# Attention over 64 graphs: scores six units ahead of the projections' count, a group of its own for the first projections, Q's weights from ScalarE's queue

## What is computed

```python
x = normal(64, 128, 512); adj = 0/1 (64, 128, 128), diagonal 1; Wq, Wk, Wv, Wo (512, 512), biases
q, k, v = heads(x @ Wq + bq), heads(x @ Wk + bk), heads(x @ Wv + bv)
scores = einsum('bhqd,bhkd->bhqk', q, k) / sqrt(32);  scores = where(adj[:, None] == 0, -inf, scores)
attn = softmax(scores);  out = einsum('bhqk,bhkd->bhqd', attn, v) @ Wo + bo
y = layernorm(x + out)          # no scale, no shift, eps 1e-5
```

## Time and profile before

| what | value |
|---|---|
| times of the runs | 904.38 us median of 3 (902.62 to 906.38) |
| the profiled execution | 906.47 us, of which its span (first to last instruction) is 904.7 us |
| mean granted TensorE clock | 0.984 |
| TensorE matmul busy | 870.5 us (96%) |
| VectorE busy | 810.5 us (90%) |
| ScalarE busy | 689.5 us (76%) |
| GpSimd busy | 272.3 us (30%) |

### The profile page before, as it was taken

The page is one execution under the profiler, slowest core; times in us unless marked ns, Lnnn a source line. Parts: engine busy times, 40 slices in busy tenths (PEclk is TensorE's granted clock), DMA queues, the critical chain, the costliest instruction groups (busy, mean ns, idle before and its releaser), DMA issues.

```text
span 904.7 us, 32198 instructions
## 1 busy us (share of the span) xinstructions
PE 870.5 (96%) x11784; PEld 607.9 (67%) x11784; DVE 810.5 (90%) x3449; ACT 689.5 (76%) x1745; POOL 272.3 (30%) x386
## 2 busy tenths in 40 slices
PE   6989999999999999999999999999999999999954
PEld 4666667776667777666777666777766677766632
DVE  5779999999999999999999999999999999999983
ACT  5777778877788877787887778877778788777761
POOL 0113233332233332323333223333232333322222
PEclk9999999999999999999999999999999999999967
DMA  8267899879789988799887779898889998778773
GB/s 302 59 129 123 161 182 183 164 152 153 151 171 179 177 169 153 136 167 182 181 159 172 144 148 169 178 177 161 145 159 159 182 178 171 156 141 158 149 135 93
DMA packets 362414, 144.98 MB, mean 160 GB/s; under 512 B 340752, under 2 KB 344848, under 8 KB 361872
## 3 DMA queue, kind: packets, MB, share of 16 engines
q1 hardware_dynamic: 362256, 142.93, 81.6%
HBM read 42.21 MB, written 16.78 MB: 65 GB/s over the span
## 4 chain that ended last, share of the span: by engine, by line
PE 93%; DVE 4%; DMA 1%; issue 1%; ACT 0%; SPq 0%; POOL 0%; POOLq 0%; DVEq 0%
PE proj_ps L605 76%; PE score_ps L605 9%; PE av_ps L605 8%; DVE masked L492 1%; DVE p_pair L479 1%; DMA w_land<-weights 1%; DVE y L518 0%; DMA aT<-a_pair 0%; DVE stats L521 0%; DVE v_parts L465 0%; DVE a_pair L458 0%; ACT probs L407 0%; ACT p_pair L417 0%; SPq L253 0%; DVE inv_sum L501 0%
## 5 line engine op out<-in xcount | busy, mean ns | idle before, releaser
L407 ACT ACTIVATE probs<-masked,minus_max 128x128 f32<-128x128 f32 x1024 | 327.0, 390 | 167.2 <-DVE minus_max L492 166.3
L492 DVE CUSTOM_DVE_ANT_0 masked<-score_ps,mask 128x128 f32<-128x128 f32 x1024 | 237.4, 287 | 45.1 <-PE score_ps L605 39.8
L479 DVE SCALAR_TENSOR_TENSOR p_pair<-probs,p_pair 128x512 f16<-128x512 f32 x256 | 197.6, 772 | 1.3 <-ACT p_pair L417 1.0
L605 PE MATMUL proj_ps<-wo_hi,aT 128*128 128x512 f16 x512 | 166.3, 387 | 2.7 <-DMA aT<-a_pair 1.6
L417 ACT ACTIVATE p_pair<-probs 128x512 f16<-128x512 f32 x256 | 161.3, 630 | 8.1
L225 POOL TENSOR_TENSOR xT_lo<-xT_raw,xT_hi 128x512 f16<-128x512 f32 x60 | 69.9, 1165 | 317.0 <-ACT xT_hi L370 317.0
L605 PE MATMUL proj_ps<-xT_hi,wq_hi 128*128 128x256 f16 x512 | 141.7, 277 | 8.6 <-DVE wq_lo L573 7.6
L605 PE MATMUL proj_ps<-xT_lo,wq_hi 128*128 128x256 f16 x512 | 141.2, 276 | 0.0
L605 PE MATMUL proj_ps<-xT_hi,wq_lo 128*128 128x256 f16 x512 | 141.2, 276 | 0.0
L605 PE MATMUL proj_ps<-xT_hi,wk_hi 128*128 128x256 f16 x512 | 140.2, 274 | 0.0
L605 PE MATMUL proj_ps<-xT_hi,wk_lo 128*128 128x256 f16 x512 | 139.6, 273 | 0.0
(11 more groups left out here) (58 smaller groups left out, 1521.2 us busy)
## 6 DMA issues: line engine op xcount, KB each, us to landing
xT_raw<-x_cols SPq DMA_DIRECT2D x32, 512.0 KB, 4.5
x_in<-x_rows SPq DMA_DIRECT2D x32, 512.0 KB, 5.4
out<-y SPq DMA_DIRECT2D x64, 256.0 KB, 4.6
adj_in<-adj SPq DMA_DIRECT2D x32, 128.0 KB, 2.9
pT<-p_pair SPq DMA_TRANSPOSE x256, 3.4
w_land<-weights SPq DMA_DIRECT2D x2, 1024.0 KB, 7.5
w_land<-weights SPq DMA_DIRECT2D x4, 256.0 KB, 4.8
x_res<-weights SPq DMA_DIRECT2D x1, 1024.0 KB, 9.3
```

The source lines that it names most:

```text
L407: ins = act.activation(probs[s % 2][:, j * S:(j + 1) * S], masked[s % 2][:, j], ACT.Exp, bias=minus_max[s % 2][:, j:j + 1], scale=-1.0)
L479: dve.scalar_tensor_tensor(out=p_pair[s % NT][:, HW:2 * HW], in0=probs[s % 2][:], scalar=P_UP, in1=p_pair[s % NT][:, 0:HW], op0=ALU.mult, ...
L492: ins = dve.tensor_tensor_reduce(masked[s % 2][:, j], score_ps[j][:, s % HC], mask[par][:, s // KC], -EXP_SCALE, 3.0e38, ALU.add, ALU.min, ...
L605: return pe.matmul(dst, lhsT, rhs, start=first, stop=last)
```

## The change

- TensorE's order is shifted: step (g, s) now scores unit 8g+s+6, attends unit 8g+s+2, and the other engines follow at fixed distances (`MAXED` 5, `TURNED` 4, `NORMED` 1). The distances between a unit's scores, its maximum, its transposes and its attention are those of before.
- The loop begins at g = -1. In that group the projections of group 0 are the banks, and the first scores stand in its step 2. The order of banks is Q0, K0, Q1, K1, V0, V1, Y of graph 1 of the group before, Y of graph 0 of this group; the last group has the scores of two units left, and six attentions.
- On VectorE `low_part_bank` is in steps 1 to 6, `low_part_attn` in 1 and 3, `make_mask` in 2, `y_and_moments` in 7 and 0. On ScalarE the high parts of attention's output are in 0 and 3, those of x in 2 and 4. On GpSimd `normalize` is in 0 and 1, `residual` in 2 and 4, the low part of x in 3 and 5. Wo's parts are made in step 7 of group -1 and steps 0 to 2 of group 0.
- Q's weights (four DMAs) are issued by ScalarE ahead of its first instruction, the others still by SyncE.
- The counters without a reader are gone.

```diff
-    TASKS = ((Q, 0), (Q, 1), (K, 0), (K, 1), (V, 0), (Y, 0), (V, 1), (Y, 1))
-    LAG = 3
+    TASKS = ((Q, 0), (K, 0), (Q, 1), (K, 1), (V, 0), (V, 1), (Y, 1), (Y, 0))
+    SCORED, MAXED, TURNED, ATTENDED, NORMED = 6, 5, 4, 2, 1
...
+    def at_work(g, s, ahead):
+        u = unit(g, s) + ahead
+        return [divmod(u, SLOTS)] if 0 <= u < NG * SLOTS else []
...
             load_xT(0)
-            load_w("q")
             sp.dma_start(b_raw[:], b_cols[:]).then_inc(bias_loaded, 16)
...
-                pool.sem_inc(gpsimd_goes, 1)
...
         def _(pool):
...
             def group(g, par):
                 for s in range(SLOTS):
-                    if s == 1 and at_least(g, 2):
+                    if s == 0 and g >= 2:
                         normalize(g - 2, 1)
+                    if s == 1 and g >= 1 and has_next(g):
+                        normalize(g - 1, 0)
...
-                    if s in (3, 6) and has_x_next2(g):
+                    if s in (3, 5) and has_x_next2(g):
...
-                    if s == 7 and at_least(g, 1):
-                        normalize(g - 1, 0)
...
         def _(act):
...
+            for c, loaded in enumerate(w_loaded["q"]):
+                act.dma_start(w_raw["q"][:, c:c + 1], w_dram[0, :, c:c + 1]).then_inc(loaded, 16)
...
         def _(dve):
...
-                dve.sem_inc(vector_goes, 1)
...
             def group(g, par):
                 for s in range(SLOTS):
-                    masked_max(g, s, par)
-                    before, slot = back(g, s, 1)
-                    if exists(before):
-                        low_part_probs(before, slot)
-                    if s > 0 and TASKS[s - 1][0] != Y and has_next(g):
+                    for unit_g, t in at_work(g, s, MAXED):
+                        masked_max(unit_g, t, unit_g % 2)
+                    for unit_g, t in at_work(g, s, TURNED):
+                        low_part_probs(unit_g, t)
+                    if 1 <= s <= N_SPLIT and has_next(g):
                         low_part_bank(g + 1, *TASKS[s - 1], nxt)
-                    if s in (2, 4) and at_least(g, 1):
-                        low_part_attn(g - 1, s // 4)
+                    if s == 1 and g >= 1:
+                        low_part_attn(g - 1, 1)
+                    if s == 3 and g >= 0:
+                        low_part_attn(g, 0)
...
-                    if s == 0 and at_least(g, 2):
-                        y_and_moments(g - 2, 1, par)
-                    if s == 6 and at_least(g, 1):
-                        y_and_moments(g - 1, 0, nxt)
...
+                    if s == (0 if has_next(g) else 3) and g >= 1:
+                        y_and_moments(g - 1, 0, nxt)
+                    if s == SLOTS - 1 and g >= 1 and has_next(g):
+                        y_and_moments(g - 1, 1, nxt)
...
         def _(pe):
...
             def group(g, par):
                 for s in range(SLOTS):
+                    if has_next(g):
+                        step_bank(g, s, par)
+                        for unit_g, t in at_work(g, s, ATTENDED):
+                            attend(unit_g, t, unit_g % 2)
+                        for unit_g, t in at_work(g, s, SCORED):
+                            scores(unit_g, t, unit_g % 2)
+                        continue
...
+            for g in range(-1, NG):
+                group(g, g % 2)
+            step_bank(LAST, 7, LAST % 2)
             pe.wait_ge(y_summed, batch(LAST - 1, 1) + 1)
             y_bank(LAST, 1)
```

More of the change, by code:

```diff
@@ L88, in wait @@
     def wait(eng, sem, value):
-        if not isinstance(value, int) or value > 0:
+        if value > 0:
             eng.wait_ge(sem, value)
-    def at_least(g, n):
-        return not isinstance(g, int) or g >= n
     def has_next(g):
-        return not isinstance(g, int) or g < LAST
+        return g < LAST
     def has_x_next2(g):
[L100 to L111, removed]
+        return g < LAST - 1
+    def at_work(g, s, ahead):
+        u = unit(g, s) + ahead
+        return [divmod(u, SLOTS)] if 0 <= u < NG * SLOTS else []
     with ExitStack() as ctx:
@@ L285, in group @@
                             load_x(g + 1, nxt)
[L286 to L289 removed]
+                    if s == 1 and g >= 2:
+                        store(g - 2, 1)
+                    if s == 2 and g >= 1 and has_next(g):
+                        store(g - 1, 0)
+                    if s == 3 and g >= 0:
+                        turn_attn(g, 0)
             load_xT(0)
[L292 removed]
             sp.dma_start(b_raw[:], b_cols[:]).then_inc(bias_loaded, 16)
@@ L356, in _ @@
             pool.wait_ge(const_made, 2)
-            all_groups(group)
-            normalize(LAST - 1, 1)
-            normalize(LAST, 0)
-            normalize(LAST, 1)
+            for g in range(-1, NG):
+                group(g, g % 2)
+            for b in range(GB):
+                normalize(LAST - 1, b)
+            for b in range(GB):
+                normalize(LAST, b)
         @block.scalar
@@ L673, in step_bank, with b_out_bank @@
                     pe.wait_ge(split_out, split_no(g + 1, *TASKS[s - 2]) + 1)
-                elif not at_least(g, 1):
-                    pe.wait_ge(split_out, split_no(g, V, s) + 1)
-                elif s == 0:
-                    pe.wait_ge(split_out, split_no(g, V, 1) + 1)
-                elif at_least(g, 2):
-                    pe.wait_ge(y_summed, batch(g - 2, 1) + 1)
-                else:
-                    pe.wait_ge(split_out, split_no(g, K, 1) + 1)
-                split_bank(g + 1, kind, i, nxt)
+                elif s == 0 and g >= 2:
+                    pe.wait_ge(y_summed, batch(g - 2, 1) + 1)
+                elif s == 0 and g == 1:
+                    pe.wait_ge(split_out, split_no(g, V, 0) + 1)
+                elif s == 0 and g == 0:
+                    pe.wait_ge(b_out_made, 1)
+                elif s == 1 and g >= 1:
+                    pe.wait_ge(y_summed, batch(g - 1, 0) + 1)
+                elif s == 1 and g == 0:
+                    pe.wait_ge(split_out, split_no(g, V, 1) + 1)
+                split_bank(g + 1, kind, i, nxt, g == -1 and i == 0)
+            def b_out_bank():
+                pe.wait_ge(w_loaded["o"][0], 16)
+                pe.wait_ge(bias_made, 2)
+                for ki in range(KC):
+                    ins = mm(b_out_ps[:], b_v_wide[:, ki], w_raw["o"][:, ki], ki == 0, ki == KC - 1)
+                ins.then_inc(b_out_mm, 1)
             def scores(g, s, par):
@@ L707, in attend @@
                     pe.wait_ge(split_out, split_no(g, V, b) + 1)
-                if isinstance(g, int) and u == 1:
-                    pe.wait_ge(b_out_made, 1)
                 for j in range(HC):
```

288 lines of the change are left out of this document (118 added, 170 removed).

## The result

The median of the changed kernel is 937.19 us (936.78 to 940.74, four runs), that of the kernel before, on the same chip, 904.49 (902.62 to 906.38). The ratio is 1.037, with a 95% interval of 1.0337 to 1.0403. The forecast of 926.5 had the sign and the cause right, but the time lies 10.7 us above it and 3.2 above the end of its range. All medians here are of fast runs alone.

A forecast was written before the change was run, and what follows sets the result against it. TensorE was taken to bound the kernel (870.5 us busy of 904.7). Start +6.9, end -13.3 and waits in the middle groups +28.5 gave +22.1 on the median: 926.5 us, range 897 to 934.

The forecast's parts named there:

- The clash of step 1: Step 1 of each group: GpSimd's residual starts 0.10 us ahead of VectorE's `low_part_attn`, which then waits 1.04 us.
- The second clash: Step 3: GpSimd's low part of x and residual meet VectorE's L479 and `low_part_attn`; 0.85 us, bounds 0 and 2.4.
- A lag up to about 0.9 is free: VectorE's step: a bank's low part ends 2.32 us in, is wanted after 3.35, so lag to about 0.9 costs nothing.
- Its last term: End of VectorE's 21.02 us sum from step 7: 2.37 us to the low part TensorE wants at step 5's start.
- The start: Ahead of group 1: more work done and late first weights; group 1 begins at 63.5, +6.9 us, bounds +4 and +10.
- 0.5 us above stands for it, bounds -1 and +1.5: Start: Wq and x landing a little later because Q's weight DMAs leave SyncE; 0.5 us.
- The end: Behind the last group's start: two score units left, last Y bank probably at half clock; 32.8 us, -13.3, bounds -16 and -10.
- The counters: Dropped `sem_inc`: 0.14 us saved ahead of VectorE's moments, bounds 0 and 0.17; 0.11 and 0.14 before L328 and L336.
- The first: Step 1: `low_part_attn` starts before the residual, GpSimd waits instead, only both ends of the kernel count; 898.0 us, chance 0.22.
- no wait arises: Middle groups: if VectorE starts first at the residual, its lags stay small and TensorE never waits; 898.0 us, chance 0.22.
- rival 3: Middle groups: TensorE's waits also bring the clock down, 48 us if once per group; 972 us, chance 0.04.
- The range: Whole kernel: 897 to 934 us; the upper end is 1.25 us of waits per group.

The follow-up runs named there:

- The experiment with the bank first: Changed kernel with VectorE's low part of the bank ahead of the low part of the probabilities in steps 2 and 4; 926.82 us, ratio 1.025.
- the run with the one small instruction: Changed kernel with one more small, unread GpSimd instruction ahead of the first residual in groups 1 to 30; 910.52 us, ratio 1.0064.

## Why the prediction was right or wrong

**The clash of step 1: right, to a hundredth.** The sum had the residual 0.10 us ahead and VectorE held for 1.04. It is 0.09 ahead and holds for 1.72 - 0.69 = 1.03. Both chains are shorter than the sum had them, 2.27 and 2.36 us from the moments for 2.35 and 2.45: the increment behind the moments, which the sum left in, had cost 0.10 us of VectorE. The margin stayed because GpSimd's normalisation is held by the low part of the probabilities, which came earlier by as much. Moving the residual 0.15 us removes the hold, so the cause is shown and not only argued. The rule of the Trainium skill, SBUF — State Buffer, section "🔬 SBUF: two separate sides", that the one which starts second is blocked for the whole instruction of the first, agrees but for 0.15 us (an overlap of 1.18 here, 1.03 longer), as the rows of before already had it; by its letter the forecast would have been nearer the time, but for a reason that is not its own.

**The second clash: nearly right.** 0.43 + 0.28 = 0.71 for 0.85.

**"A lag up to about 0.9 is free": wrong, the first failed step.** The sum took the next read-out of a bank, after 3.35 us, as the first to want K's low part. The scores of the same step want it, and they stand behind the bank and the attention, 0.33 us (one unit of scores) earlier. That makes TensorE's side 20.04 - 0.33 = 19.71. On VectorE's side three terms were off: y and moments took 1.56 (406.75 to 408.31) and not 1.65, twice, by that same increment; the second clash is 0.14 less; and the mask costs 0.17 more, since the maximum behind it now waits for its result, which no row of before showed. 21.02 - 0.18 - 0.14 + 0.17 = 20.87, and 20.87 - 19.71 = 1.16 us per group. Measured are 35.2 / 30 = 1.17 in the period, and in the waits 34.7 / 30 = 1.16 at the weight loads (0.97 at the matmuls). The forecast had 0.98. (Its last term stands as 2.37 where its own rows give 2.32; the trace has 2.41, from 419.82 to 422.23.) Groups 1 and 30 have the wait in part, as the forecast said: 27.7 and 27.3 for 27.9 in the others. This is 6.7 us of the 12.2 that were missed. The experiment with the bank first bears out the deadline: the wait leaves the scores and comes back, smaller, at the next bank.

**The start: wrong by 5.8 us, the second failed step.** "0.5 us above stands for it, bounds -1 and +1.5" priced the second issuer. It cost 3.4 us in the profiled executions, and 5.1 with the bank that fell to half the clock; on the medians 3.9. And a term was left out of the addition. The forecast counted 4.4 us of waits in the new start for 3.3 in the old and then added 6.4 for the work and 0.5 for the weights, without the 1.1 between. The traces have 4.7 for 3.3, so the counting was right, and with it the forecast would have been 64.6. Without the second issuer group 1 begins at 64.2, where the forecast's own terms, less the 0.5, give 64.1: it came within 0.7 us of 63.5 because the 0.5 stood where 1.1 was missing. (An attention is 0.26 by the forecast's own numbers and not 0.29, which is 0.15 us in all.) K's and V's loads had started behind Q's; issued from a second queue Q's last quarter lands beside them, and x later than before. The Trainium skill, DMA: Bandwidth & Descriptors, section "Issuing engines are not separate DMA queues", was weighed only as a bound on the gain. Its sentence that all issuers share the 16 DMA engines agrees with these arrivals, and it has a second side that the forecast did not read from it: what is let in earlier competes with what is wanted first. And the two banks at half the clock: one was in the sum, the second, at 1.7 us, in the bounds.

**The end: right in the sum, in part by luck.** 32.5 for 32.8, and the last scores stand 3.4 us behind, as said. But the two last Y banks took 5.28 and 4.29 for the 8.28 of before, 1.3 us more and not 2.6. About as much came from what the forecast did not have there: the two last residuals hold the low part of the attention's output once more (910.65, 1.75 for 0.69), and the low part of the probabilities ahead of it takes 1.02.

**The counters: right ahead of the moments, missed behind them.** 0.14 is what the row shows. The 0.10 behind them and the 0.12 behind the mask stood in no sum, and their return, for which 8 to 12 us were expected, made the kernel 23.2 us slower: in the changed kernel VectorE is the engine that lags, and each group has five places where nothing covers them.

**The rivals.** The first, 898.0 at 0.22, has its condition in the run with the one small instruction, and that run took 910.5. In its profiled execution group 1 begins 6.6 us later than forecast (70.1), and a group lasts 26.96 and not 26.73, 6.7 us in all, with 3.6 us of waits for K's low part and 7.2 for transposed probabilities; the end is 2.7 us shorter. So "no wait arises" was not true as it stood: the second clash and the late deadline of the scores are still there. The clock did not fall in the middle (rival 3): the granted clock from 80 to 880 us is 1.00. Its 972 should have been 974.5 by its own terms (926.5 + 48).

**The range** failed by 3 us. Its upper end was the clash at 1.25 us per group with the start at its middle. Everything mis-sized lay on the same side, and the start's own bound, 1.5 us for the weights, came from no row of two issuers.

**Open.** Some groups of the new order wait for the transposed probabilities (5.8 to 12.6 us in all, in 9 to 14 places). No experiment looked for the reason. Why one bank of the start falls to half the clock in some kernels and not in others is open too.

## What to carry to other kernels

Where two engines hold each other, find out which of the two instructions starts first, and on what margin: here 0.1 us between two chains decided 26 us, and an instruction more on the engine with time to spare was the cure. In a sum of lags, list everyone who waits for a result and take the earliest; the first waiter that comes to mind is often not it. A second queue for loads doesn't only save issue time, it also changes which bytes arrive first, and the first matmul wants the old order.

## What was not expected of the hardware

Semaphore increments behind a running instruction cost nothing (three of them: 0.80 from start to start for 0.81 without), but 0.10 to 0.14 us each ahead of VectorE's moments, which wait for its own result, behind those moments, and behind the mask; in an engine that lags they are 0.60 us per group in the rows, in a kernel that became 23.2 us slower. An instruction of GpSimd that only writes does not hold VectorE (0.52 us of memset under way, 0.68 for L439), the one with two inputs does (1.72). And a kernel's start can have a bank at half the clock (4.45 for 2.73 us) behind a wait of 1.31 us in one version and not in another with the same wait, so 1.7 us of a start are not to be promised either way.
